# One expert of 1024 inner columns per round, routing weights behind the down projection, sums on GpSimd

## The chip, the cores and the metric

The kernel runs on one core of a Trainium2 chip. Times are microseconds on the device; the shorter the better. Engines are called TensorE (PE in the rows, PEld for its weight loads), VectorE (DVE), ScalarE (ACT), GpSimd (POOL) and SyncE (SP).

## The reference

The input x is 4 batches of 1024 tokens of 128 channels. An attention layer and a layer of experts follow each other, each with a normalisation before and behind it. All is float32. Cut to what matters here:

```
x = x + ln(attn(ln(x)))            # attn(y) = heads(LN(y)) @ w_out.T + y, 16 heads of 64
x = x + ln(ffn(ln(x)))
# ffn(z), 8 experts, top 2:
probs   = softmax(z @ router)                    # 128 x 8
weights = softmax(top_2(probs)) at the two chosen experts, 0 elsewhere
for each expert e:                               # every expert is computed for every token
    fuse_e = silu(z @ gate_e) * (z @ up_e)       # 128 -> 256
out = sum_e weights[:, e] * (fuse_e @ down_e)    # 256 -> 128
```

## The kernel before

Attention comes first: eight pairs of heads by four batches make 32 groups of 16 steps, and their projected outputs are summed in `oacc`, one slab of 128 channels by 1024 tokens for each batch. Beside the steps of the last group (`first_input`) the first batch's residual, two normalisations, transposed input `zT` and routing are made. TensorE's operands are split into a high and a low part, so that each product takes three matmuls.

Then come the experts, in `expert_turns`, a loop written out by hand on each engine. For each of four batches there are 32 turns: two halves of 512 tokens, eight experts, two blocks (`ft`) of 128 inner columns. In turn v:

- TensorE makes the gate projection of turn v+1 (three matmuls of 512 columns, `hidden`, L679), at every second turn spreads the routing weights of the next expert over the partitions (`spread_weights`, L703), makes the up projection of turn v (L679) and the down projection of turn v-4 (`down`, L692), which adds up over all eight experts in one bank, `down_ps`.
- ACT computes silu of the gate (`act_sb`, L1003), copies the spread weights (`wrow_sb`) and rounds the product to its high part (`f_hi`, L986).
- GpSimd multiplies silu by the routing weight (`actw_sb`, L1677).
- DVE multiplies this by the up projection (`fuse`, L1395) and makes the low part of the product of two turns earlier (`f_lo`, L1380).

Gate and up have two banks each, used in turns. Engines run their own lists in order and meet through semaphores, so what stands ahead on an engine's list delays what follows. Between turns DVE, ACT and TensorE have other work at fixed turns: the previous batch's output (`dT` copied from `down_ps`, transposed, `take_sums`, its statistics, `nf_sb`, the final add on GpSimd) and the next batch's input: `move_projected` and the transposes of `oacc`, `attention_residual` (`y_sb`, L1159), `add_residual` (L1276), `normalise_attention` (`n_sb`), `add_tokens` (L1315), `normalise_input` (`z_sb`, L1159) in turns 17 and 18 for TensorE's transposes in turns 19 and 20 (L647), the router's logits (L662), and `route`, eight parts of small DVE steps in turns 22 to 29. TensorE transposes the routing weights (`turn_routing`, L671) in turn 31.

## Time and profile before

| | |
|---|---|
| time, median of 3 runs | 1686.27 us (1685.13 to 1686.44) |
| the profiled execution's own time | 1687.36 us |
| its span, first to last instruction | 1685.6 us |
| mean granted TensorE clock | 0.978 of 2.4 GHz |
| busy TensorE, DVE, ACT, GpSimd over the span | 93%, 77%, 72%, 77% |
| the experts, first gate to last down matmul | 1327.5 to 1671.7 us |

Busy shares are means over attention and experts, which have different limits; the windows of the batches tell more. A row of a timeline gives the start, the time from the start of the first to the end of the last of its instructions, and in brackets how long the engine was idle before, and for whom it waited.

### The profile page before, as it was taken

To read this page: it belongs to the slowest core of one execution; us is meant where nothing else is said; L and a number is where in the kernel's file an instruction comes from. 1 tells how busy PE (TensorE), PEld (TensorE's weight loads), DVE (VectorE), ACT (ScalarE), POOL (GpSimd) and SP (SyncE) were. 2 spreads that over 40 slices of the span, in tenths; PEclk is the share of its full clock that TensorE was granted. 3 is DMA by queue.
4 is the path that set the end of the run, shared out by engine and by line. 5 is a ranking of instruction groups with operands and counts; after the bars stand their busy time and mean duration, and the time that the engine had idled before them with its cause. 6 is when DMAs were issued, how large, how long until landed. Compare 5 with 4: busy or idle time off the path is not lost.

```text
span 1685.6 us, 44765 instructions
## 1 busy us (share of the span) xinstructions
PE 1566.7 (93%) x17672; PEld 1018.8 (60%) x17672; DVE 1295.9 (77%) x2799; ACT 1216.8 (72%) x2298; POOL 1306.2 (77%) x729
## 2 busy tenths in 40 slices
PE   4489999999999999999999999999997799999996
PEld 2246666666666666666666666666664576766674
DVE  6487777877777778777777777877767789989776
ACT  2477777777777777777777777777775566767665
POOL 3368999988999999889999998989973654556554
PEclk9799999999999999999999999999997899999998
DMA  4342233322322333232222333322212000000000
GB/s 125 102 134 77 77 83 91 84 77 77 83 73 77 85 85 89 77 92 71 76 80 77 89 86 90 83 71 77 71 46 77 3 1 1 1 13 1 13 1 25
DMA packets 75234, 111.28 MB, mean 66 GB/s; under 512 B 13697, under 2 KB 27265, under 8 KB 74641
## 3 DMA queue, kind: packets, MB, share of 16 engines
q1 hardware_dynamic: 75024, 108.42, 23.5%
q8 instruction: 140, 2.29, 0.6%
q14 instruction: 70, 0.57, 0.1%
HBM read 11.77 MB, written 2.10 MB: 8 GB/s over the span
## 4 chain that ended last, share of the span: by engine, by line
PE 57%; DVE 11%; issue 3%; ACT 3%; POOL 2%; DMA 1%; POOLq 0%; DVEq 0%; ACTq 0%; SPq 0%
PE psum L537 9%; PE psum L582 8%; PE psum L580 8%; PE psum L679 6%; PE psum L600 5%; PE psum L602 5%; PE psum L604 5%; PE psum L692 3%; PE psum L520 2%; DVE probs_lo L1243 2%; PE psum L563 2%; PE psum L555 1%; PE psum L703 1%; DVE fuse L1395 1%; DVE n_sb L1159 1%
## 5 line engine op out<-in xcount | busy, mean ns | idle before, releaser
L1610 POOL TENSOR_TENSOR probs_lo<-probs 128x1024 f16<-128x1024 f32 x320 | 654.5, 2058 | 142.2 <-ACT probs L936 141.4
L936 ACT ACTIVATE probs<-psum 128x512 f32<-128x512 f32 x1024 | 615.1, 603 | 186.0 <-PE psum L582 184.5
L1224 DVE CUSTOM_DVE_ANT_0 x_all<-psum,x_all 128x512 f16<-128x512 f32 x512 | 349.4, 687 | 229.3 <-PE psum L537 217.6
L600 PE MATMUL psum<-cv,probs 128*128 128x66 f16 x4096 | 476.7, 193 | 9.9 <-DVE probs_lo L1243 6.4
L602 PE MATMUL psum<-cv,probs 128*128 128x64 f16 x4096 | 476.1, 193 | 0.0
L604 PE MATMUL psum<-cv,probs_lo 128*128 128x66 f16 x4096 | 475.0, 192 | 0.0
L602 PEld LDWEIGHTS psum<-cv,probs 128*128 128x128 bf16 x4096 | 380.8, 97 | 112.4 <-issue 0.6
L600 PEld LDWEIGHTS psum<-cv,probs 128*128 128x128 bf16 x4096 | 385.5, 97 | 75.1 <-POOL probs_lo L1610 7.7
L580 PE MATMUL psum<-q_both,k_twice 128*128 128x512 f16 x1024 | 388.8, 380 | 3.6 <-ACT probs L936 3.3
L582 PE MATMUL psum<-q_max,k_ones 65*128 65x512 f16 x1024 | 391.2, 382 | 0.0
L604 PEld LDWEIGHTS psum<-cv,probs_lo 128*128 128x128 f16 x4096 | 380.2, 98 | 0.0
L923 ACT ACTIVATE x_all<-psum 128x512 f32<-128x512 f32 x512 | 305.1, 596 | 14.0 <-PE psum L537 14.0
L1677 POOL TENSOR_TENSOR actw_sb<-act_sb,wrow_sb 128x512 f32<-128x512 f32 x128 | 188.0, 1474 | 142.2 <-ACT act_sb L1003 77.5
L1243 DVE TENSOR_TENSOR probs_lo<-probs 128x1024 f16<-128x1024 f32 x192 | 291.5, 1518 | 1.9 <-ACT probs L936 1.8
L1599 POOL TENSOR_TENSOR rot<-rot,t_swapped 128x512 f32<-128x512 f32 x128 | 177.9, 1390 | 68.5 <-DMA t_swapped<-t_sin 68.3
L537 PE MATMUL psum<-x_all 128*128 128x512 f16 x512 | 196.6, 384 | 20.2 <-issue 11.0
L537 PE MATMUL psum<-qk_hi,x_all 128*128 128x512 f16 x512 | 195.9, 383 | 9.2 <-ACT x_all L923 6.7
L1605 POOL TENSOR_TENSOR qk_lo<-rot,qk_hi 128x1024 f16<-128x1024 f32 x64 | 192.1, 3004 | 0.0
L580 PEld LDWEIGHTS psum<-q_both,k_twice 128*128 128x128 f16 x1024 | 100.6, 98 | 85.6 <-ACT probs L936 5.0
L582 PEld LDWEIGHTS psum<-q_max,k_ones 65*128 65x128 f16 x1024 | 99.3, 97 | 84.5 <-issue 1.4
L1395 DVE TENSOR_TENSOR fuse<-psum,actw_sb 128x512 f32<-128x512 f32 x128 | 87.2, 681 | 49.3 <-POOL actw_sb L1677 18.2
L1380 DVE TENSOR_TENSOR f_lo<-fuse,f_hi 128x512 fp32r<-128x512 f32 x128 | 116.7, 913 | 0.0
(166 smaller groups left out, 2400.1 us busy)
## 6 DMA issues: line engine op xcount, KB each, us to landing
t_swapped<-t_sin SPq DMA_DIRECT2D x256, 128.0 KB, 2.0
k_twice<-qk_hi SPq DMA_DIRECT2D x128, 128.0 KB, 2.3
x_all<-qk_hi SPq DMA_DIRECT2D x64, 128.0 KB, 2.6
q_both<-qk_hi SPq DMA_DIRECT2D x64, 128.0 KB, 2.3
q_both<-qk_lo SPq DMA_DIRECT2D x64, 128.0 KB, 2.3
q_max<-qk_hi SPq DMA_DIRECT2D x64, 128.0 KB, 2.3
k_ones<-qk_lo SPq DMA_DIRECT2D x64, 128.0 KB, 2.3
w_raw<-w_pairs_dram SPq DMA_DIRECT2D x8, 320.0 KB, 3.2
```

The lines of the kernel that those rows point to most:

```text
L537: pe.matmul(bank, q_lone[n % 2][a][:, t * P:(t + 1) * P], keys, start=True, stop=True).then_inc(done, 1)
L580: pe.matmul(score_ps[at], k_twice[par][h][:, k0:k0 + P], q_both[par][h][:, qh * HALF:(qh + 1) * HALF], start=True, stop=False)
L582: mm = pe.matmul(score_ps[at], k_ones[h][:, k0:k0 + P], q_max[h][:, qh * HALF:(qh + 1) * HALF], start=False, stop=True)
L600: pe.matmul(acc, high[:, q * P:(q + 1) * P, 1], v[:, 0:VLO], start=opens, stop=False, skip_group_check=True)
L602: pe.matmul(acc[:, 0:DH], high[:, q * P:(q + 1) * P, 1], v[:, VLO:VW], start=False, stop=False, skip_group_check=True)
L604: mm = pe.matmul(acc, probs_lo[t % 4][:, i, q * P:(q + 1) * P], v[:, 0:VLO], start=False, stop=kp == 3 and i == 1, skip_group_check=True)
L923: act.activation(ahead[m % 2], bank[BANK_OF[("diff", n, m)]], ACT.Relu).then_inc(ahead_done, 1)
L936: act.activation(probs[s % 4][:, i, :], score_ps[tile % SCORE_BANKS], ACT.Exp, scale=SCALE).then_inc(probs_done, 1)
L1224: dve.tensor_tensor_reduce(scan_out[m % 2], bank[BANK_OF[("base", n, m)]], ahead[m % 2], 1.0, LOWEST, ALU.add, ALU.max, max_all[a][:, t:t ...
L1243: dve.tensor_tensor(probs_lo[s % 4][:].rearrange("p a n -> p (a n)"), p, p.bitcast(BF16).rearrange("p (n two) -> p n two", two=2)[:, :, 1] ...
L1605: pool.tensor_tensor(qk_lo[par][a][:], rot[a][:], qk_hi[par][a][:], ALU.subtract).then_inc(qk_lo_done, 1)
L1610: pool.tensor_tensor(probs_lo[s % 4][:].rearrange("p a n -> p (a n)"), p, p.bitcast(BF16).rearrange("p (n two) -> p n two", two=2)[:, :, 1 ...
```

## The change

A round is now one expert of one half with both blocks, a unit (64 in all). Gate and up take two banks each at a time, so each bank pair has one user. In round i the engines do: TensorE gate(i+1), up(i), the spread of unit i-2's weights, down(i-2), then what `beside_unit` holds for the round; ACT silu(i+1), the weights' copy (i-2), high part (i), then beside; DVE the product of silu and up (`combine`, 128x1024), the product of unit i-2's down projection and its weights (`scale`, to `weighed`, or to `dT` for expert 0), then beside; GpSimd adds `weighed` to `dT` for unit i-2 (`add_sums`, none for expert 0) and makes the low part of unit i (`low_hidden`). Down no longer adds up over experts in PSUM, but waits for `scaled` of the unit before. `y_sb`, `n1_sb` and `o_now` are gone: residual and token sum are fused multiply-adds (`scalar_tensor_tensor`) of 128 columns each, and the mean that the token sum leaves out (`x_shift`) is taken off in the output shift. z is made and transposed in rounds 10 and 11; routing stands in rounds 13 to 15 and round 0 of the next batch, and its weights are transposed in rounds 1 and 4. At the end of attention, gate(0) stands among the last steps, and the first up does not wait for routing.

```diff
-TURNS = EXPERT_UNITS * FT
-ROUTE_TURNS = (22, 24, 25, 26, 27, 28, 29, 29)
-SPLIT_LAG = 2
-DOWN_LAG = 4
+UNITS = B * EXPERT_UNITS
+DOWN_LAG = 2
...
-        gate_ps = [psum[:, i] for i in range(2)]
-        up_ps = [psum[:, 2 + i] for i in range(2)]
+        gate_ps = psum[:, 0:2]
+        up_ps = psum[:, 2:4]
...
+            def gate(unit):
+                b, u = divmod(unit, EXPERT_UNITS)
+                c, e = divmod(u, E)
                 if e == 0:
+                    pe.wait_ge(z_lo_done, CHUNKS * b + (c + 1))
+                if unit:
+                    pe.wait_ge(act_done, unit)
+                for ft in range(FT):
+                    mm = hidden(gate_ps[:, ft, :], wg_hi, wg_lo, e, ft, c)
+                mm.then_inc(gate_ready, 1)
+            def up(unit):
+                c, e = divmod(unit % EXPERT_UNITS, E)
+                if unit:
+                    pe.wait_ge(fuse_done, unit)
+                for ft in range(FT):
+                    mm = hidden(up_ps[:, ft, :], wu_hi, wu_lo, e, ft, c)
+                mm.then_inc(up_ready, 1)
...
+            def down(unit):
+                e = unit % E
+                if unit == 0:
+                    pe.wait_ge(down_lo, 1)
+                else:
+                    pe.wait_ge(scaled, unit)
+                pe.wait_ge(f_lo_done, unit + 1)
+                for ft in range(FT):
+                    w0 = (e * FT + ft) * D
+                    for k, (w, f) in enumerate(((wn_hi, f_hi), (wn_lo, f_hi), (wn_hi, f_lo))):
+                        mm = pe.matmul(down_ps, w[:, w0:w0 + D], f[unit % 3][:, ft, :],
+                                       start=ft == 0 and k == 0, stop=ft == FT - 1 and k == 2)
+                mm.then_inc(down_done, 1)
...
+                if u in (FIRST_TURNED, SECOND_TURNED):
...
+                    if c == 0:
+                        pe.wait_ge(route_dve, ROUTE * b + ROUTE)
+                    turn_routing(b, c)
...
+                if u == 10 and front:
+                    pe.wait_ge(res_done, CHUNKS * n + 1)
+                    pe.wait_ge(z_done, CHUNKS * n + 1)
+                    turn_tokens(0, normed, 0, z_turned)
+                if u == 11 and front:
+                    if b:
+                        pe.wait_ge(d_taken, CHUNKS * b)
+                    else:
                         pe.wait_ge(res_done, CHUNKS * n + 2)
+                    pe.wait_ge(z_done, CHUNKS * n + 2)
+                    turn_tokens(1, normed, 1, z_turned)
+                if u == 12 and front:
+                    router_logits(n)
...
+            for unit in range(UNITS + DOWN_LAG):
+                if unit + 1 < UNITS:
+                    gate(unit + 1)
+                if unit < UNITS:
+                    up(unit)
+                if unit == DOWN_LAG:
+                    pe.wait_ge(rows_done, 1)
+                if unit >= DOWN_LAG:
+                    spread_weights(unit - DOWN_LAG)
+                    down(unit - DOWN_LAG)
+                if unit < UNITS:
+                    beside_unit(*divmod(unit, EXPERT_UNITS))
...
+            for unit in range(UNITS + DOWN_LAG):
+                if unit + 1 < UNITS:
+                    activate(unit + 1)
+                if unit >= DOWN_LAG:
+                    copy_weights(unit - DOWN_LAG)
+                if unit < UNITS:
+                    high(unit)
+                    beside_unit(*divmod(unit, EXPERT_UNITS))
...
-            def move_projected(n):
-                dve.tensor_copy(o_now[:], oacc[:, bass.ds(n, 1), :].rearrange("p a n -> p (a n)")).then_inc(o_moved, 1)
-            def attention_residual(n, half):
-                normalise(batch_of(x_all, n), y_sb, batch_of(moments_x, n), rstd_x[:, bass.ds(n * TILES, TILES)],
-                          half_of(half)).then_inc(y_done, 1)
-            def add_residual(n, c):
-                tiles = slice(c * HALF_TILES, (c + 1) * HALF_TILES)
-                dve.wait_ge(y_done, CHUNKS * n + (c + 1))
-                dve.wait_ge(o_turned, CHUNKS * n + (c + 1))
-                dve.tensor_tensor(res_sb[:, tiles, :], sides(n)[1 - c].rearrange("p (t d) -> p t d", d=D), y_sb[:, tiles, :],
-                                  ALU.add).then_inc(res_done, 1)
+            def add_residual(n, half):
+                dve.wait_ge(o_turned, CHUNKS * n + (half + 1))
+                x1 = batch_of(x_all, n)
+                for t in half_of(half):
+                    at = n * TILES + t
+                    last = dve.scalar_tensor_tensor(
+                        out=res_sb[:, t, :], in0=x1[:, t, :], scalar=rstd_x[:, at:at + 1],
+                        in1=sides(n)[half][:, t % HALF_TILES * P:(t % HALF_TILES + 1) * P], op0=ALU.mult, op1=ALU.add)
+                last.then_inc(res_done, 1)
...
-                normalise(res_sb, n1_sb, ln_mv[0], ln_inv[0], half_of(half)).then_inc(n1_done, 1)
-            def add_tokens(n):
                 x1 = batch_of(x_all, n)
-                dve.wait_ge(n1_done, 2 * n + 2)
-                dve.tensor_tensor(x1, x1, n1_sb[:], ALU.add).then_inc(x1_done, 1)
-                dve.wait_ge(x1_done, n + 1)
+                for t in half_of(half):
+                    last = dve.scalar_tensor_tensor(out=x1[:, t, :], in0=res_sb[:, t, :], scalar=ln_inv[0][:, t:t + 1],
+                                                    in1=x1[:, t, :], op0=ALU.mult, op1=ALU.add)
+                last.then_inc(x1_done, 1)
+            def token_shift(n):
+                dve.tensor_tensor(x_shift[n][:], ln_mv[0][:, :, 0], ln_inv[0][:], ALU.mult).then_inc(x_shift_done, 1)
...
+            def combine(unit):
+                dve.wait_ge(up_ready, unit + 1)
+                dve.wait_ge(act_done, unit + 1)
+                if unit >= 2:
+                    dve.wait_ge(f_lo_done, unit - 1)
+                dve.tensor_tensor(fuse[unit % 2][:], up_ps, act_sb[unit % 2][:], ALU.mult).then_inc(fuse_done, 1)
+            def scale(unit):
+                chunk, e = divmod(unit, E)
+                dve.wait_ge(down_done, unit + 1)
+                dve.wait_ge(wrow_done, unit + 1)
+                if e == 0 and chunk >= CHUNKS:
+                    dve.wait_ge(d_turned, chunk - 1)
+                if e and unit >= 2 and (unit - 2) % E:
+                    dve.wait_ge(summed, sums_added(unit - 2))
+                dst = weighed[unit % 2] if e else dT[chunk % CHUNKS]
+                dve.tensor_tensor(dst[:], down_ps, wrow_sb[unit % 2][:], ALU.mult).then_inc(scaled, 1)
...
+                if u == 6 and front:
+                    inverses(0, n)
+                    add_tokens(n, 0)
+                if u == 7 and front:
+                    add_tokens(n, 1)
+                    token_shift(n)
...
+                if u in (10, 11) and front:
+                    if u == 10:
+                        inverses(1, n)
+                    normalise_input(n, u - 10)
...
+                if u == 13 and front:
+                    low_input(n, 0)
+                    route(n, 0)
+                if u == 14:
+                    if b:
+                        inverses(2, b - 1)
+                        output_shift(b - 1)
+                    take_sums(b, 0)
+                    if front:
+                        route(n, 1)
+                if u == 15 and front:
+                    route(n, 2)
+                    route(n, 3)
...
+            for unit in range(UNITS + DOWN_LAG):
+                if unit < UNITS:
+                    combine(unit)
+                if unit >= DOWN_LAG:
+                    scale(unit - DOWN_LAG)
+                if unit < UNITS:
+                    beside_unit(*divmod(unit, EXPERT_UNITS))
...
-                    pool.wait_ge(act_done, TURNS * b + (v + 1))
-                    pool.wait_ge(wrow_done, EXPERT_UNITS * b + (v // FT + 1))
-                    if not first or v >= 2:
-                        pool.wait_ge(fuse_done, TURNS * b + (v - 1))
-                    pool.tensor_tensor(actw_sb[v % 2][:], act_sb[v % 2][:], wrow_sb[v // FT % 2][:],
-                                       ALU.mult).then_inc(actw_done, 1)
...
+            def low_hidden(unit):
+                pool.wait_ge(f_hi_done, unit + 1)
...
+                pool.tensor_tensor(f_lo[unit % 3][:], fuse[unit % 2][:], f_hi[unit % 3][:].bitcast(F32),
+                                   ALU.subtract).then_inc(f_lo_done, 1)
+            def add_sums(unit):
+                total = dT[unit // E % CHUNKS]
+                pool.wait_ge(scaled, unit + 1)
+                if unit % E > 1:
+                    pool.wait_ge(summed, sums_added(unit) - 1)
+                pool.tensor_tensor(total[:], total[:], weighed[unit % 2][:], ALU.add).then_inc(summed, 1)
+            for unit in range(UNITS + DOWN_LAG):
+                if unit >= DOWN_LAG and (unit - DOWN_LAG) % E:
+                    add_sums(unit - DOWN_LAG)
+                if unit == 1:
+                    for c in range(CHUNKS):
+                        add_projected(LAST, B - 1, c)
+                if unit < UNITS:
+                    low_hidden(unit)
```

DVE's list in the first batch, around the z tiles (tile `z_sb`, of the next batch), before:

```order
2033 L1297 RECIPROCAL ln_inv<-ln_dev 128x8 [waits dev_done1]
2034 L1395 TENSOR_TENSOR fuse<-psum,actw_sb 128x512 [waits f_lo_done,actw_done,up_ready]
2035 L1380 TENSOR_TENSOR f_lo<-fuse,f_hi 128x512 [waits f_hi_done]
2036 L1159 TENSOR_SCALAR z_sb<-x_all,ln_mv,ln_inv 128x128 [waits inv_done1]
2037 L1159 TENSOR_SCALAR z_sb<-x_all,ln_mv,ln_inv 128x128 x3
2038 L1395 TENSOR_TENSOR fuse<-psum,actw_sb 128x512 [waits f_lo_done,actw_done,up_ready]
2039 L1380 TENSOR_TENSOR f_lo<-fuse,f_hi 128x512 [waits f_hi_done]
2040 L1159 TENSOR_SCALAR z_sb<-x_all,ln_mv,ln_inv 128x128 x4
```
Now:

```order
2027 L1409 TENSOR_TENSOR fuse<-psum,act_sb 128x1024 [waits f_lo_done,act_done,up_ready]
2028 L1421 TENSOR_TENSOR dT<-psum,wrow_sb 128x512 [waits wrow_done,down_done]
2029 L1316 RECIPROCAL ln_inv<-ln_dev 128x8 [waits dev_done1]
2030 L1176 TENSOR_SCALAR z_sb<-x_all,ln_mv,ln_inv 128x128 [waits inv_done1]
2031 L1176 TENSOR_SCALAR z_sb<-x_all,ln_mv,ln_inv 128x128 x3
2032 L1409 TENSOR_TENSOR fuse<-psum,act_sb 128x1024 [waits f_lo_done,act_done,up_ready]
2033 L1421 TENSOR_TENSOR weighed<-psum,wrow_sb 128x512 [waits summed,wrow_done,down_done]
2034 L1176 TENSOR_SCALAR z_sb<-x_all,ln_mv,ln_inv 128x128 x4
```
A fuse and an f_lo stood between the two halves of z, and no row of down projections; now each half stands behind a `scale` (the row that writes dT or weighed), which waits for down_done.

TensorE's list at the transposes of the first half of z (`z_sb`; wu is the up, wn the down projection), before:

```order
16227 L703 MATMUL psum<-wT,rows_r 128x512 [waits wrow_done]
16228 L679 MATMUL psum<-zT_hi,wu_hi 128x512 [waits fuse_done]
16229 L679 MATMUL psum<-zT_hi,wu_lo 128x512
16230 L679 MATMUL psum<-zT_lo,wu_hi 128x512
16231 L692 MATMUL psum<-f_hi,wn_hi 128x512 [waits f_lo_done]
16232 L692 MATMUL psum<-f_hi,wn_lo 128x512
16233 L692 MATMUL psum<-f_lo,wn_hi 128x512
16234 L647 MATMUL psum<-ident,z_sb 128x128 [waits z_done]
16235 L647 MATMUL psum<-ident,z_sb 128x128 x3
```
Now (the first row spreads the weights behind up; the six down matmuls follow):

```order
16248 L712 MATMUL psum<-wT,rows_r 128x512 [waits wrow_done]
16249 L725 MATMUL psum<-f_hi,wn_hi 128x512 [waits f_lo_done,scaled]
16250 L725 MATMUL psum<-f_hi,wn_lo 128x512
16251 L725 MATMUL psum<-f_lo,wn_hi 128x512
16252 L725 MATMUL psum<-f_hi,wn_hi 128x512
16253 L725 MATMUL psum<-f_hi,wn_lo 128x512
16254 L725 MATMUL psum<-f_lo,wn_hi 128x512
16255 L654 MATMUL psum<-ident,z_sb 128x128 [waits z_done,res_done]
16256 L654 MATMUL psum<-ident,z_sb 128x128 x3
```
The waits of the transposes are for the same tile. Before, it was made one or two turns earlier on DVE's list; now on both lists it stands at the end of the same round.

GpSimd's list from the last output sums of attention on, before:

```order
480 L1617 TENSOR_TENSOR oacc<-oacc,o_part 128x512 [waits out_copied] x2
481 L1677 TENSOR_TENSOR actw_sb<-act_sb,wrow_sb 128x512 [waits wrow_done,act_done] x2
482 L1677 TENSOR_TENSOR actw_sb<-act_sb,wrow_sb 128x512 [waits fuse_done,wrow_done,act_done] x52
483 L1677 TENSOR_TENSOR actw_sb<-act_sb,wrow_sb 128x512 [waits wrow_done,fuse_done,act_done,nf_done]
484 L1667 TENSOR_TENSOR x_all<-x_all,nf_sb 128x1024
```
Now, in the middle of the first batch:

```order
494 L1711 TENSOR_TENSOR dT<-dT,weighed 128x512 [waits summed,scaled]
495 L1702 TENSOR_TENSOR f_lo<-fuse,f_hi 128x1024 [waits f_hi_done]
496 L1711 TENSOR_TENSOR dT<-dT,weighed 128x512 [waits summed,scaled]
497 L1702 TENSOR_TENSOR f_lo<-fuse,f_hi 128x1024 [waits f_hi_done] x2
498 L1711 TENSOR_TENSOR dT<-dT,weighed 128x512 [waits scaled]
499 L1702 TENSOR_TENSOR f_lo<-fuse,f_hi 128x1024 [waits f_hi_done]
```
One op of 512 columns per turn became one of 1024 and mostly one of 512 per round; the sum waits for DVE's scale and stands ahead of the round's f_lo.

## Rows read from the trace of the kernel before

**Rows 1.** the page's first line
```profile
span 1685.6 us, 44765 instructions
```

**Rows 2.** windows of the batches: length, busy us (count) by engine, clock, DMA
```profile
1327.00:1410.00 83.00, 78.21 (x325) 55.46 (x324) 68.58 (x165) 58.40 (x97) 49.73 (x33) 1.00 0.00 1
1410.00:1499.00 89.00, 84.08 (x353) 61.13 (x352) 78.66 (x199) 62.45 (x110) 50.77 (x34) 0.98 0.02 7
...
1588.00:1665.00 77.00, 75.60 (x312) 55.28 (x311) 61.88 (x96) 50.61 (x95) 44.68 (x33) 1.00 0.03 8
```

**Rows 3.** the chain in order of time, last batch: start, us, what
```profile
1618.86 0.68 PE psum L692 x3
...
1623.60 0.68 PE psum L692 x3
```

**Rows 4.** timeline of weight loads: start, us, what, idle before and releaser
```profile
1381.31 0.42 PEld L647 LDWEIGHTS psum<-ident,z_sb 128*128 128x128 f32 x4 [1.14 <-issue]
...
1414.76 0.77 PEld L671 LDWEIGHTS psum<-ident,w_both 128*16 128x16 f32 x8 [1.85 <-issue]
...
1494.46 0.29 PEld L679 LDWEIGHTS psum<-zT_hi,wu_hi 128*128 128x128 f32 x1 [1.94 <-DVE fuse L1395]
```

**Rows 5.** groups by line and form, 1315 us to the end: busy, mean ns
```profile
L1677 POOL TENSOR_TENSOR actw_sb<-act_sb,wrow_sb 128x512 f32<-128x512 f32 x128 | 188.0, 1474 | 142.2 <-ACT act_sb L1003 77.5 <-DVE fuse L1395 51.0 <-ACT wrow_sb L990 13.7
L1380 DVE TENSOR_TENSOR f_lo<-fuse,f_hi 128x512 fp32r<-128x512 f32 x128 | 116.7, 913 | 0.0
...
L986 ACT ACTIVATE f_hi<-fuse 128x512 fp32r<-128x512 f32 x128 | 80.9, 632 | 41.3 <-DVE fuse L1395 40.8
...
L1003 ACT ACT_TABLE_LOAD x14 | 18.0, 1283 | 0.2
...
L1667 POOL TENSOR_TENSOR x_all<-x_all,nf_sb 128x1024 f32<-128x1024 f32 x4 | 10.0, 2504 | 11.9 <-ACT nf_sb L977 11.9
...
L1659 POOL TENSOR_TENSOR wn_lo<-raw_two,wn_hi 128x2048 fp32r<-128x2048 f32 x1 | 4.5, 4492 | 2.1 <-ACT wn_hi L1040 2.1
...
L1315 DVE TENSOR_TENSOR x_all<-x_all,n_sb 128x1024 f32<-128x1024 f32 x3 | 3.6, 1211 | 0.0
```

**Rows 6.** timelines of GpSimd, then of DVE, around 1375 us
```profile
1373.99 2.98 POOL L1677 TENSOR_TENSOR actw_sb<-act_sb,wrow_sb 128x512 f32<-128x512 f32 x2 [0.19 <-ACT act_sb L1003]
...
1374.50 1.34 DVE L1380 TENSOR_TENSOR f_lo<-fuse,f_hi 128x512 fp32r<-128x512 f32 x1
1375.76 2.06 DVE L1159 TENSOR_SCALAR z_sb<-x_all,ln_mv,ln_inv 128x128 f32<-128x128 f32 x4
```

**Rows 7.** one line's instructions: duration in ns, least/median/most
```profile
L1159 DVE TENSOR_SCALAR z_sb<-x_all,ln_mv,ln_inv x32: 330/334/1914, 1296.9 to 1557.7; 128x128 f32<-128x128 f32 x32
...
L1395 DVE TENSOR_TENSOR fuse<-psum,actw_sb x128: 651/680/695, 1332.5 to 1668.5; 128x512 f32<-128x512 f32 x128
```

**Rows 8.** groups by line and form, DVE alone, two routing steps
```profile
L1354 DVE TENSOR_TENSOR gap<-top 128x8 f32<-128x8 f32 x3 | 3.8, 1264 | 0.0
...
L1361 DVE TENSOR_TENSOR hot<-ids_sb,top_f 128x64 f32<-128x64 f32 x3 | 0.7, 225 | 0.1
```

**Rows 9.** the chain in order of time, end of attention to the experts
```profile
1270.34 3.84 DVE y_sb L1159 x8
...
1315.97 4.32 DVE w L1368
...
1321.57 1.87 PE psum L671 x8
```

**Rows 10.** window of 5 us in the turn to the experts
```profile
1315.00:1320.00 5.00, 0.00 (x0) 0.00 (x0) 4.86 (x6) 0.68 (x1) 4.25 (x1) 0.69 0.01 2
```

**Rows 11.** timeline of TensorE in the tail
```profile
1667.63 0.39 PE L679 MATMUL psum<-zT_lo,wu_hi 128*128 128x512 f32 x1
...
1672.80 0.66 PE L647 MATMUL psum<-ident,dT 128*128 128x128 f32 x4 [0.69 <-ACT dT L970]
```

**Rows 12.** window right behind the idle that ends at 1494.46 us
```profile
1490.00:1494.00 4.00, 2.84 (x12) 1.82 (x10) 3.91 (x25) 3.94 (x5) 1.58 (x1) 1.00 0.00 0
```

512 lines of the change are left out of this document (212 added, 300 removed).

## The prediction

> **What bounds the kernel now.** I read the windows first, then the chain, then the timelines of the engines. The diff leaves the 31 full attention groups alone, so only the last 360 us count: the end of the last group, the turn to the experts (1310 to 1327 us), four batches of experts (1327 to 1672), the tail. In the expert stage the reader sees TensorE busy nearly always, DVE busy for 78.7 of 89 us of a middle batch, GpSimd for 50.8 [rows 2]. The chain of the last batch repeats with a period of 4.74 us for two turns, one expert of one half [rows 3]. That is pure TensorE work: 18 matmuls and the one that spreads the routing weight. It contains no wait, and the change issues the same matmuls, so 16 experts cost 75.8 us per batch before and after. I call one expert of one half a unit; the new round is one unit.
>
> A middle batch takes 89 us [rows 2]. Small TensorE work beside the units (transposes, logits) is about 6.6 us of it; the other 6.8 us is waiting: 1.1 before the transposes of z, 1.9 before those of the routing weights, 1.9 for fuse while DVE does routing [rows 4], and smaller ones. From the first gate of turn 5 (1337.6) to the last up matmul (1667.6, [rows 11]) I count 18.6 us of such waiting. **This is all that a better rhythm can win in the batches.**
>
> **Part 1, the arithmetic.** Durations of before [rows 5]: GpSimd 128x512 1.3 to 1.47, DVE f_lo 0.91 in the mean (0.68 alone), ACT f_hi 0.63. The new combine is 128x1024; the nearest row on DVE is L1315 with 1.21, twice the 0.68 of the present fuse [rows 7] is the upper bound; I take 1.2. The scale of 128x512 is 0.68, of which 0.60 before the next can start. DVE per unit falls from 2 x (0.68 + 0.91) = 3.2 to 1.8. GpSimd's f_lo of 128x1024 lies between half of L1659 (2.25) and L1667 (2.50); I take 2.4. With one sum of 1.3 GpSimd needs 3.7 of 4.74 us, against 2.9 before: busier, but no bound. ACT's 1024-column ops lie between 0.63 and twice that; at 1.05 (two of them, and 0.6 for the weight's copy) it has 2.7 us per unit, less than before. No engine becomes a bound by its sum. What decides is when things are ready.
>
> **Part 2, where the waits stand.** Let T be the end of a round's down matmuls. Results are out 0.2 later. The round's combine ends at T - 0.7 (up ends 2.1 before T), f_hi at T + 0.4. DVE's scale waits for this down: T + 0.2 to T + 0.8. Only then comes what DVE does beside the unit; 2.05 us of it fit until the next combine, and 1.9 more until TensorE, at the next-but-one up, would wait.
>
> (a) z. TensorE transposes z at the end of rounds 10 and 11, and DVE makes that z at the end of the same rounds, behind scale. In before one or two turns lie between. So TensorE waits at least for scale, a reciprocal and four tensor_scalars of 0.26 each: 2.1 and 1.9 us. On top comes the lock. A z tile takes 0.33 at the least and up to 1.91 [rows 7]; undisturbed tiles follow each other by 0.26. They show an alternation too: GpSimd's first op ends at 1375.3, DVE's f_lo that had waited runs to 1375.8, GpSimd's second op then runs its 1.28, z waits for its end at 1377.0, and then four tiles follow in 0.8 [rows 6]. In the new order GpSimd has f_lo of the round ready at T + 0.5 and from round 11 also the sum just ahead of it, which starts when scale ends. Round 10 (its scale starts a new sum, so there is no add): f_lo until T + 2.9, four tiles, z at T + 3.9. Round 11: tile, sum 1.3, tile, f_lo 2.4, two tiles: T + 5.6. Together 9.5 us, in each of three batches: **+28.5**; without locks +12.
>
> (b) x1. In rounds 6 and 7 four fused multiply-adds each, x_all <- res_sb and x_all. No row shows this form against GpSimd; DVE's two-input f_lo was held in [rows 6]. If held by both GpSimd ops, each lump is 1.0 + 3.7 + small = 4.9 us; two lumps overrun 2 x 2.05 by 5.7, of which slack takes about 3: 2.75 per batch, **+8.2**; 0 if not held. The Trainium skill ("SBUF — State Buffer", Who interferes with whom) says that a DVE instruction with two SBUF inputs is shut out by a GpSimd one that reads SBUF, for its whole length; by that rule the 8.2 is right, and zero otherwise. The fused residual reads one input from PSUM, as fuse does, whose 128 cases spread over 651 to 695 ns with GpSimd at work [rows 7]: eight at 0.26 replace eight plus two of 0.6, in a round of their own, at no cost.
>
> (c) Logits in round 12 wait for ACT's second copy of z, which stands behind f_hi: T + 1.0. A table load is 1.28 [rows 5]; in round 13 ACT must load for the router's exponential after DVE's first routing step and load back before the next silu, about 1.1 late for the gate that wants its bank. Together **+6.3** for three batches.
>
> (d) Routing. Half of DVE's routing ops of a few columns take 1.26 instead of 0.22 because GpSimd holds the port [rows 8]. In the new order the lumps beside rounds 14, 15 and the next round 0 come to 5.2 (1.05 in the first batch, which has no output shift), 5.1 and 6.8 us, with a sum and an f_lo in the way of each. TensorE's transposes of the weights wait for the last step at the end of round 1. Adding combine, scale and ACT's loads for the exponential of the gap, the last step falls 8.8 us after TensorE could be there in batches 1 and 2, 5.8 in the first: **+23.4**. If nothing were held, the lumps are 1.6, 2.2 and 3.1, and the cost is 0. In before the same seam cost about 4 per batch, counted in the 18.6.
>
> (e) The clock. An idle of 1.94 us ended at 1494.5 [rows 4]; the 4 us from 1494 on have a mean granted clock of 0.57 [rows 12], that is 3.4 us at 1.2 GHz, half the speed. The idles of 4 to 6 us in (a) should do this each time: 6 x 1.7 at most; some of it falls into later waits. **+5**, bounds 0 and 20.
>
> **Part 3, the turn to the experts.** TensorE stands still from 1315 to 1320 [rows 10], until the chain's routing steps end at 1321.5; among them one op of 8 columns that took 4.3 us under GpSimd's wn_lo [rows 9]. The first gate is at 1327.5. The change puts gates 0 and 1 and up 0 ahead of that wait, routing into round 1, and the residual (3.84 us, [rows 9]) becomes about 2.1; half a batch's adds fall away too, so z of the first batch is some 3 to 4 us earlier. But combine 0 is still behind the routing on DVE, and the transposes of the last attention output and its projection stay on TensorE. The new loop should stand at its round 2 near 1328.5; before reaches the same amount of work at 1337.6. **-9**, bounds -4 and -14.
>
> **Part 4, the tail.** Before, the last sums are transposed 5.2 us after the last up matmul starts [rows 11]. Now: combine 1.2, f_hi 1.1, f_lo 2.4, six matmuls 1.4, scale 0.7, sum 1.3 and handing over 0.6: 8.9. **+3.8** with the extra step of the output shift. The later steps are the same.
>
> **Sum,** against the profiled span of 1685.6 [rows 1] (own time 1687.4, median of the runs 1686.3, so the median is the span plus 0.7): 1685.6 - 9 - 18.6 + 3.8 = 1661.8 without any wait in the new rounds. Waits: 28.5 + 8.2 + 6.3 + 23.4 + 5 = 71.4. That makes 1733. The terms were worked out one by one, and a wait at one place refills the slack of the next, so I take 6 off: 1727 as span, 1728 as median, 2.5% slower. It breaks even at 24.5 us of waits.
>
> **Rivals.**
> (R1) The port hardly matters: the short DVE ops slip in ahead of GpSimd. Then (a) is 12, (b) and (d) 0, (c) 6: 18 us of waits, 1680, 0.4% faster. It decides below 24.5 us. For it: f_lo and y were also held in before and cost little. Against: all three rows of gap took 1.26 [rows 8], and here GpSimd's ops are longer and queued two deep. Chance 0.18.
> (R2) Held once, not twice: z costs 3.9 + 3.3 per batch, the seam 3 each, (b) 0: 22 + 9 + 6 = 37, 1699. Chance 0.14.
> (R3) The clock stays at 1.2 GHz for long stretches of the three front batches. With a third of some 300 us at half speed, half of the loss hidden in waits: +50, near 1780. The expert stage of before was at 0.98 or more in every batch [rows 2], with idles below 2 us. Chance 0.08.
> The forecast, 1705 to 1765, has 0.60. The Trainium skill ("Perfetto Trace Analysis", Optimizing Scalar/DVE Operations) warns that moving work from DVE to GpSimd might not help, since they share an SBUF read port; the trace agrees as far as [rows 6] go.
>
> **How the numbers follow.** A measurement of this kernel tells 0.2%, 3.4 us, from no change. Slower: 0.60 + 0.08 + 0.12 of R2 = 0.80; same 0.04; faster 0.16. The range leaves out the better part of R1 and R3: 1682 to 1760.
>
> **What would show it.** In rounds 10 and 11 of each front batch TensorE idles 4 and 5.6 us before z's transposes, with GpSimd ops between the z tiles; idles in rounds 0 and 1 of batches 1 to 3; last-batch units at 4.74; GpSimd f_lo near 2.4; first unit near 1310. Wrong would be: z tiles together in 0.8 us right behind scale, or idles of only 2 us there (R1), or a granted clock below 0.9 in the batches (R3).

## The result, and the profile after

| | before | after |
|---|---|---|
| time, median (lowest to highest) | 1686.36 us (1685.13 to 1687.11), 4 runs | 1740.0 us (1737.75 to 1741.18), 4 runs |
| ratio, 95% interval | | 1.0317, 1.0299 to 1.0335 |
| span of the profiled execution | 1685.6 us | 1737.9 us (own time 1739.68) |

The change makes the kernel 3.2% slower; 1728 was predicted, with 1682 to 1760 as range. The windows show where: each middle batch takes 108 to 109 us, against 89 before [rows 2].

The windows of the changed kernel, by batch and tail (length, busy us and count of PE, weight loads, DVE, ACT and GpSimd, granted clock, DMA):

```profile
1324.00:1426.00 102.00, 86.95 (x346) 62.73 (x344) 61.38 (x138) 56.85 (x68) 57.91 (x31) 0.93 0.00 0
1426.00:1534.00 108.00, 89.70 (x354) 64.79 (x355) 69.69 (x164) 60.53 (x76) 56.62 (x30) 0.92 0.00 1
1534.00:1643.00 109.00, 91.16 (x353) 65.74 (x352) 69.26 (x162) 60.66 (x76) 58.92 (x31) 0.91 0.02 6
1643.00:1709.00 66.00, 66.00 (x268) 48.65 (x269) 29.38 (x47) 39.71 (x45) 47.18 (x26) 0.97 0.03 9
1709.00:1738.00 29.00, 10.99 (x28) 6.29 (x26) 10.87 (x29) 10.50 (x22) 14.38 (x8) 0.60 0.12 36
```

DVE is busy for 70 of 108 us, GpSimd for 57: nobody is full. TensorE has 90 of 108, at a mean clock of 0.92. In the last batch, which has no following batch to prepare, TensorE never stops: the new rhythm itself holds. What goes wrong is the work beside it.

The waits of the changed kernel from the start of round 2 to the end of the last up (engine, line, waited for: total us, times, longest), TensorE's weight loads alone:

```profile
PEld psum L654 <- issue: 31.2, 6, 5.3
...
PEld psum L676 <- issue: 9.4, 3, 3.2
...
PEld psum L683 <- DVE fuse L1409: 6.6, 6, 1.5
PEld psum L683 <- ACT act_sb L1007: 6.3, 3, 3.0
...
PEld psum L669 <- ACT zT L972: 4.0, 3, 1.3
...
PEld psum L683 <- issue: 2.4, 2, 1.2
```

In this order: transposes of z, transposes of the routing weights, the up that waits for the x1 rounds, the gate that waits for a late silu, logits, and the gate of the next batch. The list adds up to 59.9 us.

The groups that carry the reason (busy us, mean ns | idle before), 1324 to 1709 us:

```profile
L1702 POOL TENSOR_TENSOR f_lo<-fuse,f_hi 128x1024 fp32r<-128x1024 f32 x61 | 147.4, 2417 | 6.2 <-ACT f_hi L1013 6.0
L1409 DVE TENSOR_TENSOR fuse<-psum,act_sb 128x1024 f32<-128x1024 f32 x62 | 75.8, 1222 | 107.9 <-PE psum L683 105.7 <-DVE top_at L1383 1.8 <-DVE w_both L1402 0.2
L1711 POOL TENSOR_TENSOR dT<-dT,weighed 128x512 f32<-128x512 f32 x53 | 69.6, 1313 | 155.4 <-DVE weighed L1421 155.4
...
L1337 DVE SCALAR_TENSOR_TENSOR x_all<-res_sb,ln_inv,x_all 128x128 f32<-128x128 f32 x24 | 25.8, 1134 | 0.1
...
L1176 DVE TENSOR_SCALAR z_sb<-x_all,ln_mv,ln_inv 128x128 f32<-128x128 f32 x24 | 22.1, 981 | 0.1
...
L1287 DVE SCALAR_TENSOR_TENSOR res_sb<-x_all,rstd_x,psum 128x128 f32<-128x128 f32 x24 | 6.4, 341 | 0.0
```

Combine 1.22, f_lo 2.42 and sum 1.31 us are what was assumed (1.2, 2.4, 1.3). The reader compares the last three rows, all DVE on 128x128: the fused residual with one input in PSUM takes 341 ns, the token sum with both tensors in SBUF 1134, and the z tile 981, where undisturbed ones take 0.33 [rows 7]. It is not that GpSimd was quiet beside the residual: all 24 of its instructions overlap one of GpSimd's, and they last 336 to 343 ns.

How a z tile comes to that is in the timelines of rounds 10 and 11 of the second batch, DVE first, then GpSimd (start, us from the first to the end of the last, what, idle before):

```profile
1474.82 3.28 DVE L1176 TENSOR_SCALAR z_sb<-x_all,ln_mv,ln_inv 128x128 f32<-128x128 f32 x4
...
1485.72 0.69 DVE L1421 TENSOR_TENSOR weighed<-psum,wrow_sb 128x512 f32<-128x512 f32 x1 [0.78 <-PE psum L725]
1486.32 4.09 DVE L1176 TENSOR_SCALAR z_sb<-x_all,ln_mv,ln_inv 128x128 f32<-128x128 f32 x4
```
```profile
1474.91 2.34 POOL L1702 TENSOR_TENSOR f_lo<-fuse,f_hi 128x1024 fp32r<-128x1024 f32 x1 [1.64 <-ACT f_hi L1013]
1486.49 1.29 POOL L1711 TENSOR_TENSOR dT<-dT,weighed 128x512 f32<-128x512 f32 x1 [9.24 <-DVE weighed L1421]
1487.74 2.34 POOL L1702 TENSOR_TENSOR f_lo<-fuse,f_hi 128x1024 fp32r<-128x1024 f32 x1
```

Round 11 is the alternation that the prediction described: `scale` releases GpSimd's sum 0.17 us after the first z tile starts, the f_lo follows at once, and the four tiles need 4.09 us in place of 1.1: the first goes through in 0.34, the second lasts 1.29 beside the sum, the third 2.38 beside the f_lo, the fourth 0.33. Round 10 has one GpSimd op in the way and takes 3.28. TensorE idles 5.10 us until 1478.21 and 5.28 us until 1490.53, and what follows runs at the lower clock of 1.2 GHz: 4.4 us of work, to 1482.6, and 5.7 us, to 1496.2. Windows from this stretch (the first begins while TensorE still idles):

```profile
1476.00:1480.00 4.00, 1.75 (x7) 1.59 (x8) 2.10 (x4) 0.00 (x0) 1.25 (x1) 0.50 0.00 0
1480.00:1484.00 4.00, 4.00 (x12) 2.75 (x10) 0.29 (x1) 1.03 (x1) 0.00 (x0) 0.67 0.00 0
...
1492.00:1496.00 4.00, 4.00 (x11) 3.14 (x10) 0.00 (x0) 1.02 (x1) 0.00 (x0) 0.50 0.00 0
```

The last round with an output shift, on DVE, in the tail:

```profile
1709.05 1.23 DVE L1322 SCALAR_TENSOR_TENSOR out_shift<-ln_mv,ln_inv 128x8 f32<-128x8 f32 x1
1710.32 2.29 DVE L1326 TENSOR_TENSOR out_shift<-out_shift,x_shift 128x8 f32<-128x8 f32 x1
```

and what ACT and TensorE do with it (both rows are the first behind the wait):

```profile
1712.65 1.65 ACT L998 ACTIVATE nf_sb<-moe_sb,out_shift,ln_inv 128x128 f32<-128x128 f32 x4 [3.92 <-DVE out_shift L1326]
...
1714.83 0.28 PEld L712 LDWEIGHTS psum<-wT,rows_r 16*128 16x128 f32 x1 [3.69 <-ACT wrow_sb L1019]
```

Two ops of eight columns, 0.17 us each when free, take 3.5 us. DVE's own last combine, behind them, starts at 1713.14, 4.0 us after the last up matmul starts (1709.17). ACT's normalisation stands in its queue ahead of the weights' copy and the high part, and TensorE waits 3.69 us.

One row of the prediction was shown wrongly: [rows 12] has the window of 1490 to 1494. The window meant, from the same answer on the kernel before, is this; its clock of 0.57 is the number in the prediction:

```profile
1494.00:1498.00 4.00, 3.54 (x9) 2.86 (x10) 3.93 (x8) 2.23 (x4) 2.08 (x2) 0.57 0.00 0
```

### The profile page after: what moved, and what is told of

It reads as the page before. It is cut to its first block, busy times and chain, and to the rows that moved or that the text cites. A ratio compares the mean times of both kernels' runs of the same rounds, so it can differ in the third digit from the quotient of the medians.

```text
span 1737.9 us, 44375 instructions
## 1 busy us (share of the span) xinstructions
PE 1586.8 (91%) x17672; PEld 1033.4 (59%) x17672; DVE 1242.4 (71%) x2651; ACT 1208.6 (70%) x2164; POOL 1342.0 (77%) x721
## 4 chain that ended last, share of the span: by engine, by line
PE 57%; DVE 10%; ACT 5%; issue 3%; POOL 2%; DMA 0%; POOLq 0%; DVEq 0%; ACTq 0%
PE psum L544 8%; PE psum L589 8%; PE psum L587 8%; PE psum L683 8%; PE psum L609 5%; PE psum L607 5%; PE psum L611 5%; PE psum L725 3%; PE psum L527 2%; DVE probs_lo L1260 2%; PE psum L570 2%; DVE fuse L1409 1%; PE psum L562 1%; DVE z_sb L1176 1%; ACT f_hi L1013 1%
## 5 line engine op out<-in xcount | busy, mean ns | idle before, releaser
L950 ACT ACTIVATE x_all<-psum 128x512 f32<-128x512 f32 x512 | 304.6, 595 | 13.6 <-PE psum L544 13.4
L1260 DVE TENSOR_TENSOR probs_lo<-probs 128x1024 f16<-128x1024 f32 x192 | 296.9, 1547 | 1.8 <-ACT probs L963 1.8
L1711 POOL TENSOR_TENSOR dT<-dT,weighed 128x512 f32<-128x512 f32 x56 | 73.4, 1311 | 161.0 <-DVE weighed L1421 160.9
L1702 POOL TENSOR_TENSOR f_lo<-fuse,f_hi 128x1024 fp32r<-128x1024 f32 x64 | 154.5, 2414 | 11.9 <-ACT f_hi L1013 11.8
L1409 DVE TENSOR_TENSOR fuse<-psum,act_sb 128x1024 f32<-128x1024 f32 x64 | 78.2, 1222 | 108.6 <-PE psum L683 106.5
```

What stands on the lines that cost most here:

```text
L950: act.activation(ahead[m % 2], bank[BANK_OF[("diff", n, m)]], ACT.Relu).then_inc(ahead_done, 1)
L1260: dve.tensor_tensor(probs_lo[s % 4][:].rearrange("p a n -> p (a n)"), p, p.bitcast(BF16).rearrange("p (n two) -> p n two", two=2)[:, :, 1] ...
```

## The experiments

All ratios are to the kernel before on the same chip. "Waits of z" are TensorE's idles before the transposes of z, per batch.

**e1, GpSimd steps aside for z.** In rounds 10 and 11 of the front batches GpSimd waits for the z tiles before it takes its sum and low part.

```diff
+            def yield_port(unit):
+                b, u = divmod(unit, EXPERT_UNITS)
+                if b < B - 1 and u in (10, 11):
+                    pool.wait_ge(z_done, CHUNKS * (b + 1) + (u - 9))
```

> GpSimd alone is changed: in rounds 10 and 11 of each front batch it waits for the half of z that DVE makes in that round before it starts its sum and its low part. Same work, nothing left out. Theory A (TensorE waits for z because z stands in its own round, and GpSimd's two ops get between the z tiles through the port): the four tiles run in 0.8 us, TensorE's waits before the transposes of z fall from 5.1 and 5.3 us to about 2.3 and 2.0, 18 us for three batches, and with less time at half clock some 22: near 1718. Theory B (the order of the lists alone makes these waits, the port does not matter): the waits stay, the time stays at 1738 to 1742, or gets longer since GpSimd is later.

Measured: 1717.02 us, ratio 1.0186 (1.0169 to 1.0203). The waits of z fall to 2.96 and 2.30; all others stay. DVE's four z tiles of round 10, in the second batch:

```profile
1469.31 1.11 DVE L1176 TENSOR_SCALAR z_sb<-x_all,ln_mv,ln_inv 128x128 f32<-128x128 f32 x4
```

Same tiles, same place in DVE's queue, 1.11 in place of 3.28 us, with nothing changed but GpSimd's moment. Some 5 us of 10.4 per batch are the port's (the SBUF port that DVE and GpSimd share, as the prediction has it); the rest is order (scale, reciprocal, four tiles behind the down).

**e2, GpSimd steps aside for all of DVE's short work**: as e1, and in rounds 6 and 7 (x1), 13 to 15 and 0 (routing, output shift).

```diff
+                    if u == 6:
+                        pool.wait_ge(x1_done, CHUNKS * n + 1)
+                    if u == 7:
+                        pool.wait_ge(x_shift_done, n + 1)
...
+                    if u == 13:
+                        pool.wait_ge(z_lo_done, CHUNKS * n + 1)
+                    if u == 15:
+                        pool.wait_ge(route_dve, ROUTE * n + 7)
+                if 0 < b < B and u == 14:
+                    pool.wait_ge(inv_done[2], 3 * (b - 1) + 3)
+                if 0 < b < B and u == 0:
+                    pool.wait_ge(route_dve, ROUTE * b + ROUTE)
```

> As before with z, and in rounds 6, 7 (x1), 13 (low part of z), 14 (output shift), 15 (the gap of routing) and 0 (last routing step) GpSimd also waits until DVE's lump of that round is done. Same work. Theory A: the 2.2 us per batch at rounds 8 and 9 go (6.5 us), the lumps of the seam shrink by some 2 us each, the output shift no longer holds ACT up in the tail (3 us): 1700 to 1708. Theory B: 1735 to 1745. If only the z rounds matter: 1718, as with z alone.

Measured: 1686.58 us, ratio 1.0007 (0.9997 to 1.0016): no different from before, and below the 1700 to 1708 expected. Eight waits a batch on GpSimd, without a single op less, give back the whole loss. The groups of e2 for the two kinds of 128x128 work:

```profile
L1337 DVE SCALAR_TENSOR_TENSOR x_all<-res_sb,ln_inv,x_all 128x128 f32<-128x128 f32 x24 | 7.6, 378 | 0.1
L1176 DVE TENSOR_SCALAR z_sb<-x_all,ln_mv,ln_inv 128x128 f32<-128x128 f32 x24 | 6.7, 341 | 0.1
```

1134 and 981 ns became 378 and 341. TensorE's listed waits from round 2 to the last up fall from 59.9 to 23.3 us. The estimate was short mainly in the clock: its mean is 0.98 over these 333 us, where the changed kernel has 0.93 over 385.

**e11, the seam alone**: e2 without the waits for x1 and z.

> The changed kernel with GpSimd's waits at the routing seam alone (rounds 13, 14, 15 and 0 of e2, not those for x1 and z). Theory A (the seam term (d) is the port's): waits of 3.25, 3.05, 3.06 before the transposes of the weights, 2.95 twice for silu and 3.7 in the tail go, as in e2; z waits 5.1 and 5.3 and x1 waits 2.2 stay. Sum of waits gone about 17, clock 2 to 4: 1719 to 1721. Rival B (the gains of e2 need the x1 and z waits too, since a late z carries over to the seam): 1728 or more.

Measured: 1717.11 us, ratio 1.019 (1.0176 to 1.0204), 2 below the expected 1719 to 1721. z waits (5.1 and 5.3) and x1 stay. With e1 it splits the loss. By spans of the profiled executions it is 19.2 us for z, 23.7 for the seam with 3.4 in the tail, and 12.9 left of e2's 55.8; but e1's profiled execution was its slowest. By the ratios, from several executions each, it is 22 for z, 21 for the seam and 9 left of 52, beside 6.6 us of x1 waits. The two routing steps that show the seam, first the changed kernel, then e11:

```profile
L1386 DVE CAST top_f<-top_at 128x64 f32<-128x64 uint32 x3 | 7.1, 2375 | 0.0
...
L1326 DVE TENSOR_TENSOR out_shift<-out_shift,x_shift 128x8 f32<-128x8 f32 x2 | 4.6, 2311 | 0.1
```
```profile
L1386 DVE CAST top_f<-top_at 128x64 f32<-128x64 uint32 x3 | 0.6, 189 | 0.0
...
L1326 DVE TENSOR_TENSOR out_shift<-out_shift,x_shift 128x8 f32<-128x8 f32 x2 | 0.3, 166 | 0.1
```

**e3, ACT's order**: the first half of the output's normalisation from round 14 to 15, behind the silu that it held up.

```diff
-                if u == 14 and b:
+                if u == 15 and b:
                     normalise_output(b - 1, 0)
```

> ACT alone is changed: the first half of the output normalisation stands beside round 15 instead of round 14, so that ACT does not wait for DVE's output shift with silu, weight copy and high part queued behind it. Same work. Theory A (with ACT's queue as a part of the seam): the gate's wait of 2.95 us for silu at the seams of batches 1 and 2 goes, and some 4 us of the tail: about 1731. Rival (DVE's routing chain alone sets the seam): the waits move to the transposes of the routing weights, only the tail gains: 1736.

Measured: 1734.33 us, ratio 1.0289 (1.0272 to 1.0306), between the two. The wait of 2.95 for silu is gone, but one of 1.2 for fuse and one of 3.23 for the next silu stand there, and the one before the weights' transposes fell from 3.05 to 1.6 in the third batch and under 0.7 in the last. Moving one reader of a late value moves the wait; it does not make the value earlier.

**e4, z's transposes half a round later**: from the end of rounds 10 and 11 to the middle of 11 and 12, between up and down.

```diff
+            def inside_unit(b, u):
+                n = b + 1
+                if u == 11 and n < B:
+                    pe.wait_ge(z_done, CHUNKS * n + 1)
+                    turn_tokens(0, normed, 0, z_turned)
...
```

> TensorE alone is changed: the transposes of the two halves of z stand in the middle of rounds 11 and 12, behind the up matmuls, instead of at the end of rounds 10 and 11. Gate and up, 2.75 us, then run while DVE makes z. Same work. Theory A: each of six waits shrinks by 2.75 us, 16 us, and with the clock about 20: near 1720, with waits of 2.4 and 2.5 us left, which are the GpSimd ops between the tiles. Theory B (order alone): a half of z needs 2.1 us behind scale, so the waits vanish altogether, 31 us: near 1707.

Measured: 1715.76 us, ratio 1.0176 (1.0159 to 1.0193), waits of z 2.05 to 2.6. That is near theory A's 2.4 and 2.5 and its 1720, not B's none and 1707: gate and up of a round, 2.8 us, cover half of a z that is late by 5.

**e5, both**: e2 with z's transposes as in e4 and the logits in the middle of round 13.

> The kernel of e2 (GpSimd steps back for DVE's short work) with TensorE's transposes of z moved from the end of rounds 10 and 11 to the middle of rounds 11 and 12, and the logits to the middle of round 13. Theory A (what is left of the z waits in e2, 2.63 and 2.30 us per batch, is only order: z is made at the end of the round in which it is wanted; half a round, 2.8 us, is more than that): z waits and the logits wait of 1.31 vanish in all three batches, 3 x 6.2 = 18.7 us less than e2's 1686.6, so 1668, about 1% under the kernel before. Rival B (as e4 showed without the GpSimd waits, where the order move took 2 x 2.9 per batch and left 2.2 each: DVE and ACT pass the delay on to the next round): a gain of half that, 1677. If GpSimd's held low parts become late, slower than e2.

Measured: 1662.39 us (1661.39 to 1663.52), ratio 0.9867 (0.9852 to 0.9882), 1.3% faster than the kernel before and better than theory A's 1668. Its windows, three front batches, the last and the tail:

```profile
1324.00:1407.00 83.00, 82.17 (x355) 61.37 (x354) 49.56 (x145) 57.98 (x70) 55.77 (x31) 1.00 0.00 1
1407.00:1490.00 83.00, 82.92 (x354) 61.93 (x353) 51.49 (x161) 60.27 (x77) 55.66 (x31) 0.98 0.00 1
1490.00:1572.00 82.00, 81.45 (x353) 60.41 (x352) 51.59 (x162) 60.24 (x77) 57.74 (x32) 1.00 0.02 7
1572.00:1634.00 62.00, 62.00 (x256) 45.57 (x255) 27.00 (x43) 38.57 (x45) 48.57 (x26) 1.00 0.03 9
1634.00:1660.00 26.00, 9.12 (x29) 5.29 (x28) 8.01 (x30) 10.51 (x23) 14.32 (x8) 0.66 0.13 40
```

TensorE is busy 82 of 83 us, a middle batch takes 82 to 83 where before took 89, and the clock is full or nearly so (0.98 to 1.00; in e2 0.96 to 0.98 in the front batches). That may be why it beats theory A by 5 us; no run separates it. DVE's busy time in a middle batch is 51.5 in place of 69.7 us: 18 us of "busy" were standing at the port.

**e6, f_lo in two pieces**: the changed kernel with GpSimd's low part as two instructions of 128x512.

```diff
+                for ft in range(FT):
+                    last = pool.tensor_tensor(f_lo[unit % 3][:, ft, :], fuse[unit % 2][:, ft, :],
+                                              f_hi[unit % 3][:, ft, :].bitcast(F32), ALU.subtract)
+                last.then_inc(f_lo_done, 1)
```

> The changed kernel with GpSimd's f_lo of 128x1024 as two instructions of 128x512. Theory A (DVE and GpSimd alternate instruction by instruction, so in a burst each waiting DVE op pays one GpSimd instruction until GpSimd's list of the round is through): the single holds fall from 2.3 to 1.2, but as many more are paid; the sum of GpSimd's work in the way is the same. z waits within 1 us of 5.1 and 5.3, seam within 1 us; time 1735 to 1745. Rival B (a burst is held once, for the instruction that is running, then it goes through): each burst is about 1.2 us shorter, some 10 per kernel, 1728 or less.

Measured: 1730.97 us, ratio 1.0271 (1.0256 to 1.0287), in neither range and nearer to B. Where DVE has four tiles in a row, A is right: z waits 4.99 and 5.16, as each tile meets the next piece. Where DVE has one or two short ops, B is right: in the two output shifts of the batches the second step takes 1204 ns in place of 2311, so the silu wait is 1.82 in place of 2.95 and the tail's 2.61 in place of 3.69. Both fit one reading: each DVE op that can be held pays the rest of the GpSimd instruction that it meets, and GpSimd's queue moves on by one meanwhile.

**e7, the fusion alone**, put into the kernel before (no y, no n1, one multiply-add per tile, an extra step of the output shift).

> The kernel before with only the fused residual and token sum (no mean subtracted, one multiply-add per tile, one more step in the output shift). Part 3 of the prediction: z of the first batch 3 to 4 us earlier, and in the traces the last routing step of the first batch ends at 1316.7 in the changed kernel against 1321.5 before. Theory A: the first gate comes 4 us earlier, batches as before, tail 0.4 later: 1682 to 1683, 0.2% faster. Rival B (the multiply-adds with two SBUF inputs are held by GpSimd's products in the batches, and z comes later there; or the op of 4.3 us under wn_lo takes the whole gain): 1686 to 1689.

Measured: 1680.4 us (1678.31 to 1682.38), ratio 0.9974 (0.9963 to 0.9986), 0.3% faster. The first gate starts at 1322.3 in place of 1327.5, and the experts keep the same rhythm. In it the fused token sum has a mean of 597 ns: held here too, but behind GpSimd ops of half the length, with slack.

**e8, the late start**: the changed kernel with gate 0 behind the whole routing of the first batch.

```diff
-                if s == STEPS:
-                    pe.wait_ge(probs_done, KEY_TILES * GROUPS)
-                    pe.wait_ge(stage_lo, 1)
-                    gate(0)
...
-            pe.wait_ge(route_dve, 1)
+            pe.wait_ge(route_dve, ROUTE)
             pe.wait_ge(stage_lo, 2)
+            gate(0)
```

> The changed kernel with the first gate behind the routing of the first batch, as before. In the changed kernel routing ends at 1316.7 on DVE, the first combine starts at 1318.7. Theory A: gate 0, gate 1 and up 0 (2.8 to 4.2 us) then lie behind 1316.7, the first combine starts near 1322, round 2 some 3 us later, plus 1 for the clock after a longer idle: 1743 to 1744, so of the 13.7 us of the turn about 4 are the early gates and the rest is the earlier end of routing and the work taken off the seam. Rival B (the early gates are the whole term of 9): 1749. Rival C (DVE bounds the turn anyway): 1740, no change.

Measured: 1748.11 us, ratio 1.0374 (1.036 to 1.0388). Round 2 starts at 1332.15 in place of 1323.91, 8.2 us later: rival B. Against before the turn gained 13.7 us (1337.6 to 1323.9); 8.2 are the early gates, and e7's 5.2 us is the earlier z. The two make 13.4.

**e9, the tail**: e5 with DVE making the last f_lo and the last sum.

> The kernel of e5 with DVE, which is idle there, making the last f_lo and the last sum in GpSimd's place. In e5 the last down waits 1.79 us for a f_lo of 2.35 that stands behind a sum on GpSimd, and the last transposes wait 2.91 us. Theory A (Part 4: the tail is a chain through GpSimd's slow ops): f_lo about 1.9 us earlier, sum 0.7 in place of 1.3: 2.5 to 3 us less, 1659.5. Rival B (DVE's f_lo is held by GpSimd's f_lo and sum in front of it and ends where GpSimd's did): only the 0.6 of the sum, 1662.

Measured: 1660.45 us, ratio 0.9856 (0.9841 to 0.9871). Against e5's 0.9867 that is not told apart; rival B fits. DVE on its three last steps of the chain:

```profile
1639.17 2.22 DVE L1620 TENSOR_TENSOR f_lo<-fuse,f_hi 128x1024 fp32r<-128x1024 f32 x1 [0.86 <-POOL f_lo L1715]
...
1643.74 0.69 DVE L1425 TENSOR_TENSOR weighed<-psum,wrow_sb 128x512 f32<-128x512 f32 x1 [1.76 <-PE psum L725]
1644.47 1.93 DVE L1624 TENSOR_TENSOR dT<-dT,weighed 128x512 f32<-128x512 f32 x1
```

The f_lo is held first, by GpSimd's sum that ends at 1640.30. The last sum takes 1.93 us on DVE, more than GpSimd's 1.3: GpSimd, freed of it, is in its output sum of 128x1024 by then (1643.51 to 1645.85), and DVE's sum ends only behind it, at 1646.40. Work that is moved from GpSimd to DVE meets the same port.

**e10, the clock alone**: the changed kernel with 20 unused matmuls in each wait of z.

```diff
+            def fill(side):
+                for k in range(20):
+                    pe.matmul(side_ps[side], wg_hi[:, 0:P], zT_hi[:, 0:HALF], start=True, stop=True)
...
+                    fill(0)
...
+                    fill(1)
```

> The changed kernel with 20 matmuls of 128x512 (about 4.6 us, results unused, overwritten by the transposes) put into TensorE's waits of 5.1 and 5.3 us before the transposes of z in rounds 10 and 11. Theory A (a wait of 5 us costs its own length and then a stretch of 6.8 us at 1.2 GHz): the six stretches at the z waits disappear, half-clock time falls from 87 to some 45 us, and the time falls by 8 to 12 us, to 1730. Rival B (the half-clock stretches lie in work that is hidden behind the next waits, so they cost nothing): 1738 to 1740, the z waits' ends do not move.

Measured: 1729.06 us, ratio 1.0264 (1.025 to 1.0278). The windows around the z rounds of the second batch, which answer to those of the changed kernel:

```profile
1476.00:1480.00 4.00, 4.00 (x17) 2.86 (x16) 1.23 (x1) 1.62 (x2) 0.00 (x0) 1.00 0.02 4
1480.00:1484.00 4.00, 4.00 (x20) 3.27 (x19) 3.25 (x4) 1.55 (x2) 2.48 (x2) 1.00 0.00 0
1484.00:1488.00 4.00, 3.67 (x19) 2.79 (x18) 1.54 (x2) 0.33 (x1) 1.20 (x1) 1.00 0.00 0
```

The clock is 1.00 where it was 0.50 and 0.67. The tiles of z are held as before (3.20 and 4.18 us for four), so that it is the clock that differs; more matmuls make the kernel faster by 0.5%, 9 to 11 us, by the ratios or by the medians. That is theory A, 1.5 to 1.8 us for each of the six idles.

## Why the prediction was right, and which terms were off

The sum with measured terms, against before's span: 1685.6 - 13.7 (turn) - 18.6 (waits of before gone) + 73.9 (waits and clock from round 2 at 1323.9 to the last up at 1709.2: 385.3 us, less the 311.4 that before's 330.0 are without its 18.6) + 10.7 (tail: 28.7 us behind the last up, 18.0 before) = 1737.9. The predicted sum was 1727, right in sign, mechanism and size within 11 us, and R1 to R3 are out. That it came so near is in part luck, for its errors cancel in part: it was too short by 2.7 us for z, 9.0 for the clock, 6.9 for the tail and the 6 taken off for overlap, and too long by 1.6 for x1, 7.6 for logits and seam and 4.7 for the turn. Its break-even of 24.5 us sets a median against a span; span against span it is 23.8. By its steps:

- **The rhythm** held: the last batch's rounds follow each other at 4.75 us (4.74 predicted), and durations were as taken.
- **(a) z**, 9.5 per batch: measured 10.4. Round 11 was worked out as 5.6 and is 5.3; round 10 as 3.9 and is 5.1. The step that failed is "GpSimd has f_lo of the round ready at T + 0.5": it waits 1.64 us for f_hi, since ACT loads tables beside that round, and so starts 0.09 us after the first tile instead of being half through. e1 and e4 show both parts, port and order; of "without locks +12" e1 leaves 15.8, for the order alone costs 2.96 in round 10 where 2.1 was taken.
- **(b) x1**, 2.75 per batch: measured 2.2, six waits of 6.6 together. e2 and e11, which differ in x1 and z, show that it is the port; the residual with its PSUM input was free, as said. The Trainium skill ("SBUF — State Buffer", Who interferes with whom) says that a DVE instruction contends with GpSimd if it has two SBUF inputs and GpSimd's reads SBUF, or if it runs in a two-port mode, for which it names `tensor_scalar`, and not otherwise. The trace agrees: 1134 ns with two SBUF inputs, 981 for z's `tensor_scalar`, 341 with the second input in PSUM.
- **(c) and (d)**, 6.3 + 23.4: logits 4.0, silu 6.3, the next batch's gate 2.4, weights' transposes 9.4, together 22.1 of 29.7. The seam was right as a place and as a mechanism: in e11 the waits before the transposes of the weights are 1.4 us in all and those for silu 0.5. What was missing is the path: the output shift, held for 3.5 us, delays ACT's normalisation, and that the silu in the same queue; its delay then takes part of what the prediction put before the transposes (e3).
- **(e) Clock**, +5: mis-sized. The listed waits are 59.9 of the 73.9 us; 14 is left, 1.3 of it a wait in round 2 and the rest, by the granted clock, nearly all half speed. e10 gives 9 to 11 us back from the z rounds alone, 1.5 to 1.8 for each idle, which is the 1.7 of the prediction. What failed is that it halved this to 5, "some of it falls into later waits", and that it left out the seam: behind its waits the windows of 4 us from 1520, 1534, 1629 and 1643 have 0.57 to 0.60.
- **Minus 6 for overlap** came out in size and not in its reason: (a) to (d) less 6 are 60.4 us, the listed waits 59.9. With the z and seam terms taken out one at a time (e1, e11) the gains nearly add up to e2, so that no wait of z refilled slack of the seam. The shortfall lies inside (c) and (d), where one wait takes part of the next, and that the two sizes agree is luck.
- **Part 3, the turn**, -9: measured -13.7, at the edge of its bounds. The two parts were seen as one; e7 and e8 price them at 5.2 and 8.2, and they add.
- **Part 4, the tail**, +3.8: measured +10.7, and nearly all of it lies ahead of the last transposes. From the last up matmul to them it takes 15.3 us, not 8.9; "the later steps are the same" holds within 0.6 us (13.4 against 12.8). What failed is the sum of 8.9: it starts combine right behind the up, but the output shift of the third batch falls into the last rounds and is held for 3.5 us, so that DVE starts combine 4.0 us after the start of the last up matmul (and ACT copies the weights of the last two downs late); it lets f_lo follow f_hi, but GpSimd has a sum of 1.3 us ahead of it; and it takes 1.4 us for six matmuls, which run at 1.2 GHz (0.60 in the tail's window) and take 2.9. In e11, where the shift is not held, the wait of 3.69 is 0.5, but others of 1.41 and 1.82 stand behind it and the tail is shorter by 3.4 us.

Left open: of the 55.8 us by which e2's span is shorter, its listed waits account for 36.6 and its tail for 4.3. The 15 left go with the clock (0.98 against 0.93, an estimate of some 41 us less at half speed from these clocks over 385 and 333 us), but no run holds the clock alone fixed in e2. x1's waits were never taken out alone. Whether the tail can be made as short as before was tried once (e9, 24.4 us against 18.0 from the last up) and not reached.

## What to carry to other kernels

When work goes from DVE to GpSimd, ask not whether either is full but which short DVE ops on the path of the bounding engine will meet a long GpSimd op. Of the kinds that were held here (two tensors in SBUF, z's `tensor_scalar`, a cast) each op costs the rest of that instruction, whatever its own size; those that read one tensor from PSUM were not held. GpSimd can be told to wait for them at no cost where it has slack: here such waits were worth 52 to 53 us, and with an order half a round looser the same change is 1.3% faster than before. A wait of 5 us on TensorE costs its length and then a stretch at half speed, so price the two together. Price the parts of a change apart: the fusion alone was a gain that the sum hid.
